# Output projection in plain fp32, and another warm-up of small matmuls, in a fused cross-attention and expert kernel

## Chip, cores and metric

One Trainium2 chip, one of its cores. The time is that of one execution on the device in microseconds; the kernel before ran three times.

## The reference

32 batches, each a matrix of 128 channels by 1024 positions, all fp32. A block of windowed cross-attention is followed by a mixture of rank-64 experts.

```
def xattn(x, cond, Wq, bq, Wk, bk, Wv, bv, Wo, bo):     # x: LayerNorm(x), cond: ctx
    q, k, v = Wq @ x + bq, Wk @ cond + bk, Wv @ cond + bv
    # 8 heads of 16 channels; position t sees the 16 keys from t-8 to t+7
    dots = einsum('bhdt,bhdtw->bhtw', qh, k_win) * hd ** -0.5
    out = einsum('bhtw,bhdtw->bhdt', softmax(dots), v_win)
    return Wo @ out + bo
x = x + xattn(layernorm(x), ctx, ...)
y = layernorm(x)
w = top-2 gate weights of softmax(y @ gate_w.T)          # 8 experts
x = x + sum over e of w[e] * (y @ A[e].T @ B[e].T)
```

## The kernel before

Every batch goes through one pipeline of five engines, each with its program written out by hand in the order of its instructions; semaphores join them. A step (`step(later, ahead, cur, prev, old)`) works on five batches at once: `later` is loaded and normalised, `ahead` gets its q and k projections and its first chunk of scores, `cur` its v projection, scores and softmax, `prev` its attention output and output projection `project_o`, and `old` the experts. `head` brings batches b0 to b3 to that point; then a step follows for each batch, the last ones with fewer batches. TensorE's program is unrolled in full (`loops=0`); the other engines loop over two steps.

Large products are made of float32r operands. A value is split in a high part, rounded to float32r (ScalarE, `*_hi`), and the rest (GpSimd or VectorE, `*_lo`), and `one_pass` multiplies high by high, high by low and low by high. `project_pass` does so for a 128x128 weight in `w_split` and half of 1024 columns, so a projection (`project_q`, `project_k`, `project_v`, `project_o`) is six float32r matmuls of 128x512 into `bank_c`. `down` (16 products, 128x264 or 128x256) and `up` (8 products, 128x512) are the experts' two matrices. The rest is plain fp32: a chunk of scores is 64 matmuls of 32x32, a chunk of weighted values 18 of 64x96 or less, and there are 12 transposes a batch. A plain fp32 statement other than a transpose stands in the profile as two matmuls and two weight loads: the 64 of a chunk of scores are x128, the 28 of the warm-up x56.

The order on TensorE in a step: v of `cur` (which waits for `x1_done`, the residual of `old`), weighted chunk 2 of `prev`, the first transposes, scores chunk 1, q of `ahead`, half of `down(0, ·)`, weighted chunk 3 of `prev`, the other half, scores chunk 2, half of `down(1, ·)`, weighted chunk 0 of `cur`, the other half, k of `ahead`, scores chunk 3, the second transposes, `project_o(prev)`, weighted chunk 1, half of `up`, scores chunk 0 of `ahead`, the other half of `up`. Each chunk opens with its waits (`open_scores`, `open_weighted`).

The attention output `attn` is written in four chunks, by ScalarE for even heads (`even_heads`) and by VectorE, which adds the odd ones (`join_heads`, `attn_done`). `attention_hi` (ScalarE, L676) and `attention_lo` (GpSimd, L1114) split it into `attn_split` for `project_o`. `even_heads(b, 0)` waits for `attn_lo` of the batch before, since it overwrites `attn`. VectorE's `residual` (L954) adds `project_o`'s result to x and `second_norm` follows it. At the end of the head, VectorE's order is `join_heads(b1, 0)`, `first_norm(b3)`, `residual(b0)`, `second_norm(b0)`, `scores_shift(b2, 0)`.

`warm_up(28)` runs 28 fp32 matmuls of 128x128 on a zeroed buffer before the data is there. SyncE issues the loads in a fixed order: x and ctx of b0, the constants, the weights in nine pieces (piece 0 holds Wq, Wk, Wv and Wo in 128x512), then `load_x(b1)`, which waits for `normal_lo(b0)` (L1120), and so on; in a step `place_v` (v_diag), `load_resid`, `load_x`, `load_ctx`, `store`.

Of the kernel before, what the change touches and what calls it, by code (L numbers as in the profile page):

```python
# [29 lines left out]
F32 = mybir.dt.float32  # L30
# [6 lines left out]
P = 128  # L37
# [7 lines left out]
KT = 32  # L45
# [53 lines left out]
def build(nc, x, ctx, wqkvo, biases, down_w, up_w, ident_in, mask_in, consts_in, out):  # L99
    with ExitStack() as stack:  # L100
        def sb(name, shape, dt=F32):
            return stack.enter_context(nc.sbuf_tensor(name, shape, dt))
# [4 lines left out]
        def sem(name):  # L107
            return stack.enter_context(nc.semaphore(name))
# [23 lines left out]
        attn = sb("attn", [P, T])  # L132
        attn_split = sb("attn_split", [P, 2, T], F32R)
        mid_split = sb("mid_split", [P, 2, T], F32R)
# [23 lines left out]


        small_in, consts_in_sbuf = sem("small_in"), sem("consts_in_sbuf")  # L160
        weights_in = [sem(f"weights_in{n}") for n in range(9)]
# [17 lines left out]
        exp_done, xt_hi = sem("exp_done"), sem("xt_hi")  # L179
        mask_set, ctx_hi, attn_hi = sem("mask_set"), sem("ctx_hi"), sem("attn_hi")  # L180
        xn_done, xn2_done = sem("xn_done"), sem("xn2_done")
# [7 lines left out]
        result_done, xt_lo = sem("result_done"), sem("xt_lo")  # L189
        attn_lo, rstd1, xn_lo = sem("attn_lo"), sem("rstd1"), sem("xn_lo")  # L190
        prob_done, rstd2, ctx_lo = sem("prob_done"), sem("rstd2"), sem("ctx_lo")
# [17 lines left out]
        def first(b):  # L209

            return isinstance(b.j, int) and b.j + b.c == 0
# [34 lines left out]
        def _(sp):  # L246
# [47 lines left out]
            def head(b0, b1, b2, b3):  # L294
# [7 lines left out]
                sp.dma_start(ident[:], ident_in).then_inc(small_in, 16)  # L302
                sp.dma_start(mask[:], mask_in).then_inc(small_in, 16)
                load_piece(2)
                load_piece(3)
# [34 lines left out]
        def _(pe):  # L340
# [126 lines left out]
            def project_o(b, free):  # L467

                pe.wait_ge(attn_hi, b.count(1, 1))
                pe.wait_ge(attn_lo, b.count(1, 1))  # L470
                pe.wait_ge(*free)
                for n in range(6):
                    last = project_pass(n, bank_c, 3, attn_split)
                    if n % 3 == 2:
                        last.then_inc(o_done, 1)

            def warm_up(matmuls):

                pe.wait_ge(prob_zero, 1)
                for n in range(matmuls):  # L480
                    nc.tensor.matmul(bank_c[:, 0:P], prob[:, 0:P], prob[:, 0:P], start=True, stop=True)

            def head(b0, b1, b2, b3):

                warm_up(28)
                first_masks()
# [40 lines left out]
            def step(later, ahead, cur, prev, old):  # L527
# [19 lines left out]
                if ahead:  # L547
                    project_q(ahead, (v_out, cur.count(1, 1)))
                pe.wait_ge(xt_lo, old.count(2, 1))
                if old.c == 0:  # L550
# [3 lines left out]
                if prev and cur:  # L554
                    open_weighted(prev, 3)
                    weighted_chunk(prev, 3)
                pe.wait_ge(xt_lo, old.count(2, 2))
                for f in range(4, FK):
# [20 lines left out]
                if cur:  # L579
                    project_o(prev, (k_out, ahead.count(1, 1)) if ahead else (v_out, cur.count(1, 1)))  # L580
                    open_weighted(cur, 1)
                    weighted_chunk(cur, 1)
                pe.wait_ge(ht_lo, old.count(1, 1))
                for e in range(EK):
                    up(0, e)
                if ahead:
                    pe.wait_ge(mask_set, ahead.count(CHUNKS, -1))
                    scores_chunk(ahead, 0)
# [7 lines left out]
        def _(act):  # L596
# [14 lines left out]
            def even_heads(b, m):  # L611

                act.wait_ge(pv_done, b.count(CHUNKS, m + 1))
                if m == 0 and b.c >= 1:
                    act.wait_ge(attn_lo, b.count(1, 0))
                src = bank_b[2 + m % 2][:].rearrange("p (n h i) -> p n h i", h=2, i=QT)
# [49 lines left out]
            def context_hi(b):  # L666

                act.wait_ge(ctx_in[b.parity], b.turn(1))
                nc.scalar.activation(ctx_split[:, 0, :], ctx_of(b), ACT.Copy).then_inc(ctx_hi, 1)  # L669

            def attention_hi(prev):

                act.wait_ge(attn_done, prev.count(CHUNKS, CHUNKS))
                if prev.c >= 1:
                    act.wait_ge(o_done, prev.count(2, 0))
                nc.scalar.activation(attn_split[:, 0, :], attn[:], ACT.Copy).then_inc(attn_hi, 1)  # L676

# [25 lines left out]
            def head(b0, b1, b2, b3):  # L703
# [41 lines left out]
                write_mask(b1, 2)  # L745
                attention_hi(b0)
                exponentials(b1, 3)
# [5 lines left out]
            def step(later, ahead, cur, prev, old):  # L753
# [19 lines left out]
                if prev:  # L773
                    even_heads(prev, 3)
                    attention_hi(prev)
                if cur:
# [293 lines left out]
        def _(pool):  # L1070
# [39 lines left out]

            def attention_lo(prev):

                pool.wait_ge(attn_hi, prev.count(1, 1))
                nc.gpsimd.tensor_tensor(attn_split[:, 1, :], attn[:], attn_split[:, 0, :].bitcast(F32),  # L1114
                                        ALU.subtract).then_inc(attn_lo, 1)

            def normal_lo(later):
# [5 lines left out]
            def head(b0, b1, b2, b3):  # L1123
# [22 lines left out]
                context_lo(b2)  # L1146
                attention_lo(b0)
                split_lo(7)
# [5 lines left out]
            def step(later, ahead, cur, prev, old):  # L1154
# [5 lines left out]
                if ahead:  # L1160
                    context_lo(ahead)
                if prev:
                    attention_lo(prev)
                if cur:
# [58 lines left out]
```

## Time and profile before

| | us |
|---|---|
| median of 3 runs | 1057.43 (1052.64 to 1060.89) |
| the profiled execution | 1057.9 |
| its span, first to last instruction | 1056.1 |
| TensorE matmul busy | 1011.5 (96%) |
| TensorE weight load busy | 869.8 (82%) |
| VectorE busy | 872.8 (83%) |
| ScalarE busy | 582.5 (55%) |
| GpSimd busy | 432.5 (41%) |

The mean granted clock of TensorE is 0.987 of full speed. A matmul's end is modelled and matmuls overlap in the pipeline, so the distance between two starts says more than the length of one. Idle time is shown in square brackets before an instruction, with what ended it; "issue" means that no wait is visible.

### The profile page before, as it was taken

How to read it: one execution, taken by the hardware profiler on the slowest of the kernel's cores; microseconds unless marked ns; L12 is line 12 of the kernel's file. 1: busy time of each engine (PE TensorE's matmuls, PEld its weight loads, DVE VectorE, ACT ScalarE, POOL GpSimd, SP SyncE). 2: the span in 40 equal slices, each digit the busy share in tenths (PEclk: the TensorE clock that was granted, in tenths of full speed). 3: DMA queues.
4: the chain of work that ended last, by engine and by line, in shares of the span. 5: the costliest groups of instructions: out<-in, count | busy, mean ns of one | idle time of the engine just before them, and what ended most of it. 6: DMA issues, size and time to landing. Idle time of an engine off the chain costs nothing.

```text
span 1056.1 us, 54652 instructions
## 1 busy us (share of the span) xinstructions
PE 1011.5 (96%) x24508; PEld 869.8 (82%) x24508; DVE 872.8 (83%) x1889; ACT 582.5 (55%) x812; POOL 432.5 (41%) x373
## 2 busy tenths in 40 slices
PE   6879999999999999999999999999999999999987
PEld 5768888888888888888888888888888888888866
DVE  3778888888888888888889888889888888888852
ACT  6666555556555556555555555556555555654420
POOL 7773434434434434343434343444343443443210
PEclk9899999999999999999999999999999999999998
DMA  7232333322333322223332223332233332222210
GB/s 271 78 80 86 83 84 103 103 66 81 82 83 103 103 81 71 76 84 103 103 85 71 84 83 91 103 103 58 87 84 83 103 103 73 76 81 64 64 41 40
DMA packets 157721, 92.47 MB, mean 88 GB/s; under 512 B 139728, under 2 KB 139856, under 8 KB 157520
## 3 DMA queue, kind: packets, MB, share of 16 engines
q1 hardware_dynamic: 157520, 89.25, 28.9%
q8 instruction: 192, 3.15, 1.2%
q14 instruction: 9, 0.07, 0.0%
HBM read 55.16 MB, written 16.78 MB: 68 GB/s over the span
## 4 chain that ended last, share of the span: by engine, by line
PE 87%; issue 5%; DVE 5%; ACT 2%; DMA 1%; POOL 1%; DVEq 0%; SPq 0%
PE bank_a L351 35%; PE bank_b L401 18%; PE bank_c L351 16%; PE bank_b L380 13%; PE bank_a L410 5%; DVE stats L815 1%; DMA raw<-x 1%; DMA prob_t<-ctx 0%; DVE h_sb L875 0%; DVE row_max L886 0%; DVE row_sum L900 0%; DVE pick L861 0%; DVE resid_pair L954 0%; POOL x_split L1120 0%; ACT x_split L688 0%
## 5 line engine op out<-in xcount | busy, mean ns | idle before, releaser
L401 PEld LDWEIGHTS bank_b<-prob_t,v_diag 64*64 64x64 f32 x4608 | 192.0, 134 | 50.3 <-issue 41.9
L401 PE MATMUL bank_b<-prob_t,v_diag 64*64 64x96 f32 (+2 forms) x4608 | 211.4, 239 | 12.6 <-issue 12.2
L351 PE MATMUL bank_a<-down_split,mid_split 128*128 128x264 f32 (+1 forms) x1536 | 213.7, 289 | 1.5 <-DVE mid_split L934 1.4
L351 PEld LDWEIGHTS bank_a<-down_split,mid_split 128*128 128x128 f32 x1536 | 193.4, 188 | 8.6 <-DVE mid_split L934 2.3
L1091 POOL TENSOR_TENSOR prob<-prob,row_inv 128x512 f32<-128x512 f32 x128 | 134.2, 1049 | 159.0 <-DVE row_inv L904 157.2
L351 PE MATMUL bank_a<-up_split,ht_split 128*128 128x512 f32 x768 | 196.6, 407 | 2.8 <-DVE ht_split L941 2.8
L380 PEld LDWEIGHTS bank_b<-k_sb,q_diag 32*32 32x32 f32 x16384 | 155.0, 105 | 43.9 <-issue 36.7
L380 PE MATMUL bank_b<-k_sb,q_diag 32*32 32x32 f32 x16384 | 170.6, 195 | 10.7 <-issue 6.7
L351 PEld LDWEIGHTS bank_a<-up_split,ht_split 128*128 128x128 f32 x768 | 142.8, 192 | 33.7 <-DVE ht_split L941 3.3
L1114 POOL TENSOR_TENSOR attn_split<-attn,attn_split 128x1024 fp32r<-128x1024 f32 x32 | 76.1, 2378 | 145.6 <-ACT attn_split L676 145.6
L913 DVE STREAM_TRANSPOSE prob_t<-prob 128x768 f32<-128x768 f32 x128 | 122.9, 961 | 0.9 <-POOL prob L1091 0.9
L624 ACT ACTIVATE prob<-prob 128x512 f32<-128x512 f32 x128 | 80.2, 627 | 67.0 <-DVE prob L892 67.0
L1120 POOL TENSOR_TENSOR x_split<-raw,x_split 128x1024 fp32r<-128x1024 f32 x32 | 76.9, 2404 | 96.5 <-ACT raw L688 96.5
L618 ACT ACTIVATE attn<-bank_b,consts 128x256 f32<-128x256 f32 x128 | 59.5, 465 | 90.1 <-PE bank_b L401 90.1
L886 DVE TENSOR_REDUCE row_max<-bank_b 128x16 f32<-128x512 f32 x128 | 86.7, 677 | 19.9 <-PE bank_b L380 19.5
L351 PE MATMUL bank_c<-ctx_split,w_split 128*128 128x512 f32 x372 | 98.6, 401 | 4.3 <-POOL ctx_split L1097 4.3
L1097 POOL TENSOR_TENSOR ctx_split<-raw,ctx_split 128x1024 fp32r<-128x1024 f32 x30 | 72.0, 2398 | 58.5 <-ACT ctx_split L669 58.5
L892 DVE TENSOR_TENSOR prob<-bank_b,row_max 128x512 f32<-128x512 f32 x128 | 88.5, 691 | 4.4
L900 DVE TENSOR_REDUCE row_sum<-prob 128x16 f32<-128x512 f32 x128 | 85.3, 666 | 2.1 <-ACT prob L624 1.9
L1105 POOL TENSOR_TENSOR rstd<-var_eps,consts 128x1 f32<-128x1 f32 x64 | 35.2, 550 | 124.9 <-DVE var_eps L824 124.9
L834 DVE SCALAR_TENSOR_TENSOR attn<-bank_b,consts,attn 128x256 f32<-128x256 f32 x128 | 58.3, 457 | 32.4 <-ACT attn L618 32.4
L351 PEld LDWEIGHTS bank_c<-ctx_split,w_split 128*128 128x128 f32 x372 | 68.8, 191 | 17.8 <-issue 4.3
(79 smaller groups left out, 1316.2 us busy)
## 6 DMA issues: line engine op xcount, KB each, us to landing
v_diag<-v_t SPq DMA_DIRECT2D x128, 132.0 KB, 3.3
raw<-x SPq DMA_DIRECT2D x32, 512.0 KB, 4.5
resid_pair<-x SPq DMA_DIRECT2D x32, 512.0 KB, 4.0
out<-resid_pair SPq DMA_DIRECT2D x32, 512.0 KB, 4.3
raw<-ctx SPq DMA_DIRECT2D x30, 512.0 KB, 3.3
stage<-down_w SPq DMA_DIRECT2D x2, 528.0 KB, 10.6
q_diag<-up_w SPq DMA_DIRECT2D x2, 512.0 KB, 5.7
prob_t<-up_w SPq DMA_DIRECT2D x2, 512.0 KB, 7.2
```

The source lines that it names most:

```text
L351: return nc.tensor.matmul(dst, st[:, s, st_cols], mv[:, m, mv_cols], start=start and n == 0, stop=stop and n == 2)
L380: last = nc.tensor.matmul(bank_b[m % 2][rows, t * KT:(t + 1) * KT], q_diag[rows, cur.parity, n, :], keys[rows, n * QT:n * QT + KT], start= ...
L401: last = nc.tensor.matmul(bank_b[2 + m % 2][rows, lo * PW:hi * PW], value_blocks(b)[rows, n, :], prob_t[rows, at:at + (hi - lo) * KT], sta ...
L624: nc.scalar.activation(weights_of(m), weights_of(m), ACT.Exp).then_inc(exp_done, 1)
L886: nc.vector.tensor_reduce(row_max[:, cols], scores, AX_X, ALU.max).then_inc(max_done, 1)
L892: nc.vector.tensor_tensor(weights_of(m), scores, row_max[:, cols].unsqueeze(2).broadcast_to([P, CT, KT]), ALU.subtract).then_inc(shifted, 1)
L900: nc.vector.tensor_reduce(row_sum[:, cols], weights_of(m), AX_X, ALU.add).then_inc(sum_done, 1)
L913: nc.vector.transpose(prob_t[:, m * PC:(m + 1) * PC], prob[:, m % 2 * PC:(m % 2 + 1) * PC]).then_inc(prob_t_done, 1)
L1091: nc.gpsimd.tensor_tensor(weights_of(m), weights_of(m), row_inv[:, cols].unsqueeze(2).broadcast_to([P, CT, KT]), ALU.mult).then_inc(prob_d ...
L1097: nc.gpsimd.tensor_tensor(ctx_split[:, 1, :], ctx_of(b), ctx_split[:, 0, :].bitcast(F32), ALU.subtract).then_inc(ctx_lo, 1)
L1114: nc.gpsimd.tensor_tensor(attn_split[:, 1, :], attn[:], attn_split[:, 0, :].bitcast(F32), ALU.subtract).then_inc(attn_lo, 1)
L1120: nc.gpsimd.tensor_tensor(x_split[:, 1, :], raw[:], x_split[:, 0, :].bitcast(F32), ALU.subtract).then_inc(xn_lo, 1)
```

## The change

The output projection takes `attn` and a plain copy `wo` of Wo as fp32 operands: two statements of 128x512, one for each half, instead of six float32r ones. `attn_split`, `attention_hi` and `attention_lo` are gone, and with them their passes on ScalarE and GpSimd. `wo` is loaded by a DMA of its own (128 rows of 512 bytes), issued after the mask and before piece 2. `project_o` waits for `attn_done`; `even_heads(b, 0)` waits for `o_done` of the batch before where it waited for `attn_lo`. The warm-up is 60 matmuls of 32 columns by 32 instead of 28 of 128 by 128. Four places on TensorE wait for more semaphores than before: both halves of `down(0, ·)` for `xt_hi` beside `xt_lo`, `up` for `ht_hi` beside `ht_lo`, and scores chunk 0 of `ahead` through `open_scores` for `k_out` and `q_out` beside `mask_set`.

```diff
+        wo = sb("wo", [P, P])
-        attn_split = sb("attn_split", [P, 2, T], F32R)
...
                 sp.dma_start(mask[:], mask_in).then_inc(small_in, 16)
+                sp.dma_start(wo[:], wqkvo[:, 3 * P:4 * P]).then_inc(wo_in, 16)
                 load_piece(2)
...
             def project_o(b, free):
-                pe.wait_ge(attn_hi, b.count(1, 1))
-                pe.wait_ge(attn_lo, b.count(1, 1))
+                pe.wait_ge(attn_done, b.count(CHUNKS, CHUNKS))
+                if first(b):
+                    pe.wait_ge(wo_in, 16)
                 pe.wait_ge(*free)
-                for n in range(6):
-                    last = project_pass(n, bank_c, 3, attn_split)
-                    if n % 3 == 2:
-                        last.then_inc(o_done, 1)
+                for n in range(2):
+                    half = slice(n * HALF, (n + 1) * HALF)
+                    nc.tensor.matmul(bank_c[:, half], wo[:], attn[:, half],
+                                     start=True, stop=True).then_inc(o_done, 1)
...
-                    nc.tensor.matmul(bank_c[:, 0:P], prob[:, 0:P], prob[:, 0:P], start=True, stop=True)
+                    nc.tensor.matmul(bank_c[0:KT, 0:KT], prob[:, 0:KT], prob[:, 0:KT], start=True, stop=True)
...
-                warm_up(28)
+                warm_up(60)
...
+                pe.wait_ge(xt_hi, old.count(2, 1))
                 pe.wait_ge(xt_lo, old.count(2, 1))
...
+                pe.wait_ge(xt_hi, old.count(2, 2))
                 pe.wait_ge(xt_lo, old.count(2, 2))
...
+                pe.wait_ge(ht_hi, old.count(1, 1))
                 pe.wait_ge(ht_lo, old.count(1, 1))
...
-                    pe.wait_ge(mask_set, ahead.count(CHUNKS, -1))
+                    open_scores(ahead, 0)
                     scores_chunk(ahead, 0)
...
                 if m == 0 and b.c >= 1:
-                    act.wait_ge(attn_lo, b.count(1, 0))
+                    act.wait_ge(o_done, b.count(2, 0))
```

The definitions and calls of `attention_hi` (ScalarE) and `attention_lo` (GpSimd) are removed in the head and in the step.

## Rows read from the trace of the kernel before

**Rows 1.** The summary: its span, queues, and the chain by engine.

```profile
span 1056.1 us, 54652 instructions
...
q8 instruction: 192, 3.15, 1.2%
...
PE 87%; issue 5%; DVE 5%; ACT 2%; DMA 1%; POOL 1%; DVEq 0%; SPq 0%
```

**Rows 2.** Windows: PE, PEld, DVE, ACT, POOL busy (count), clock, DMA share, GB/s.

```profile
480.00:580.00 100.00, 97.72 (x2469) 84.39 (x2469) 86.13 (x184) 57.28 (x80) 40.45 (x35) 1.00 0.31 89
```

**Rows 3.** All waits of TensorE from 80 to 1000 us.

```profile
PE bank_b L401 <- issue: 10.5, 19, 1.2
PE bank_b L380 <- issue: 2.4, 5, 0.8
PE bank_a L410 <- DVE h_sb L875: 1.0, 4, 0.3
```

**Rows 4.** Instructions in order of time, TensorE, one step: start us, us.

```profile
550.50 1.57 PE L401 MATMUL bank_b<-prob_t,v_diag 64*64 64x64 f32 x36
552.00 1.74 PE L351 MATMUL bank_a<-down_split,mid_split 128*128 128x264 f32 x12
553.67 1.29 PE L380 MATMUL bank_b<-k_sb,q_diag 32*32 32x32 f32 x128
...
556.49 0.66 PE L401 MATMUL bank_b<-prob_t,v_diag 64*64 64x64 f32 x10
557.69 1.23 PE L401 MATMUL bank_b<-prob_t,v_diag 64*64 64x96 f32 x26 [0.54 <-issue]
...
561.88 1.28 PE L380 MATMUL bank_b<-k_sb,q_diag 32*32 32x32 f32 x128
...
563.51 1.64 PE L351 MATMUL bank_c<-attn_split,w_split 128*128 128x512 f32 x6
565.08 1.58 PE L401 MATMUL bank_b<-prob_t,v_diag 64*64 64x64 f32 x36
566.58 3.02 PE L351 MATMUL bank_a<-up_split,ht_split 128*128 128x512 f32 x12
569.53 1.29 PE L380 MATMUL bank_b<-k_sb,q_diag 32*32 32x32 f32 x128
```

**Rows 5.** The same at the start: the masks' weight loads.

```profile
11.32 0.30 PEld L346 LDWEIGHTS bank_b<-mask,ident 128*128 128x128 f32 x2
...
11.86 0.19 PEld L346 LDWEIGHTS bank_b<-mask,ident 128*128 128x128 f32 x1 [0.24 <-issue]
...
12.29 0.19 PEld L346 LDWEIGHTS bank_b<-mask,ident 128*128 128x128 f32 x1 [0.24 <-issue]
```

**Rows 6.** The chain that ended last: start us, us, what.

```profile
12.30 8.28 DMA raw<-x
...
63.59 0.48 ACT attn L618
```

**Rows 7.** DMA issues of SyncE in the step of rows 4.

```profile
551.07 0.43 SPq L286 DMA_DIRECT2D resid_pair<-x  x1
551.83 0.34 SPq L270 DMA_DIRECT2D raw<-x  x1
```

**Rows 8.** Groups of instructions by line: count, busy us, mean ns, idle before.

```profile
L1114 POOL TENSOR_TENSOR attn_split<-attn,attn_split 128x1024 fp32r<-128x1024 f32 x32 | 76.1, 2378 | 145.6 <-ACT attn_split L676 145.6
...
L848 DVE CAST top_atf<-top_at 128x2 f32<-128x2 uint32 x32 | 67.8, 2120 | 1.1
```

**Rows 9.** Instructions in order of time, the tail.

```profile
1017.39 1.61 PE L351 MATMUL bank_c<-attn_split,w_split 128*128 128x512 f32 x6 [1.56 <-issue]
1018.43 1.41 DVE L954 SCALAR_TENSOR_TENSOR resid_pair<-bank_c,bias,resid_pair 128x512 f32<-128x512 f32 x2 [1.12 <-PE bank_c L351]
```

**Rows 10.** The same, TensorE, the last stretch of the head.

```profile
64.69 1.64 PE L351 MATMUL bank_c<-attn_split,w_split 128*128 128x512 f32 x6
...
67.76 1.65 PE L351 MATMUL bank_c<-ctx_split,w_split 128*128 128x512 f32 x6
```

More of the change, by code:

```diff
@@ L157, in build @@
         bank_c = psum("bank_c", T)
+        wo_in = sem("wo_in")
         small_in, consts_in_sbuf = sem("small_in"), sem("consts_in_sbuf")
@@ L179, in build @@
         exp_done, xt_hi = sem("exp_done"), sem("xt_hi")
-        mask_set, ctx_hi, attn_hi = sem("mask_set"), sem("ctx_hi"), sem("attn_hi")
+        mask_set, ctx_hi = sem("mask_set"), sem("ctx_hi")
         xn_done, xn2_done = sem("xn_done"), sem("xn2_done")
@@ L189, in build @@
         result_done, xt_lo = sem("result_done"), sem("xt_lo")
-        attn_lo, rstd1, xn_lo = sem("attn_lo"), sem("rstd1"), sem("xn_lo")
+        rstd1, xn_lo = sem("rstd1"), sem("xn_lo")
         prob_done, rstd2, ctx_lo = sem("prob_done"), sem("rstd2"), sem("ctx_lo")
@@ L669, in context_hi @@
                 nc.scalar.activation(ctx_split[:, 0, :], ctx_of(b), ACT.Copy).then_inc(ctx_hi, 1)
[L671 to L676, printed above, removed]
             def gap_exponential(old):
@@ L745, in head @@
                 write_mask(b1, 2)
-                attention_hi(b0)
                 exponentials(b1, 3)
@@ L774, in step @@
                     even_heads(prev, 3)
-                    attention_hi(prev)
                 if cur:
@@ L1109, in rows_norm @@
                                         rstd[:, which:which + 1], ALU.mult).then_inc(ready[1], 1)
[L1111 to L1115, printed above, removed]
             def normal_lo(later):
@@ L1146, in head @@
                 context_lo(b2)
-                attention_lo(b0)
                 split_lo(7)
@@ L1161, in step @@
                     context_lo(ahead)
-                if prev:
-                    attention_lo(prev)
                 if cur:
```

## Prediction

> **What bounds the kernel now.** I read the summary first. The chain that ended last is 87% TensorE, 5% "issue" and 5% VectorE, in a span of 1056.1 us [rows 1]. Then a window of the middle: in 100 us TensorE is busy 97.72 us at full granted clock, VectorE 86.13, ScalarE 57.28, GpSimd 40.45 [rows 2]. So between about 80 and 1000 us only two things move the end: what TensorE does, and the little time in which it does nothing. Third, the waits of that stretch: TensorE waited for another engine for 1.0 us in all, but 10.5 + 2.4 us for "issue", in 24 places [rows 3]. "Issue" is time in which no wait is visible. Fourth, one step in order of time: each group of matmuls follows the last without a gap, except that the 36 of `weighted_chunk(cur, 0)` break after the 10th [rows 4]. Ten of them take 10/36 of the 1.50 us that the whole group takes elsewhere (551.99 − 550.50), 0.42 us, and the eleventh starts 1.20 us after the first, so 0.78 us is lost where the view, whose matmul ends overlap, counts 0.54. With these 0.24 us more for each, the 24 gaps of [rows 3] are 12.9 + 24 × 0.24 = 18.7 us. A gap under 0.24 us isn't listed at all; I add 1.6 us for some ten steps that have one. That is 20.3 us, or 0.70 us in each of 29 steps.
>
> **What the gap is.** 192 instruction packets bring 3.15 MB [rows 1]: 16.4 KB each. TensorE has 24,508 matmuls and as many weight loads, 49,016 / 192 = 255 for a packet. So a packet is a block of 256 instructions of 64 bytes. From the code one step has 764 matmul records (24 for the four projections, 12 transposes, 48 down, 24 up, 512 scores, 144 weighted), hence 1,528 instructions; one more wherever a matmul waits for more than one semaphore (eight places: four `open_weighted`, q, k, o and the first transposes) makes 1,536 = 6 blocks exactly. That is why the gap stands behind the same 10th matmul in step after step. Going back 256 instructions from it (20 of the weighted chunk, 24 of `down`, 212 of scores) the block before began 44 instructions into scores chunk 2, at 553.67 + 0.21 = 553.88. The scores run at 256 instructions in 1.22 us, so this block is used up by 556.91, in 3.0 us, and the next is there at 557.69, 3.8 us after this one was entered. In this reading the next block is asked for on entry and takes 3 to 4.2 us (the upper end is the longest gap, 1.2 us, on 3.0). The other short block of a step ends in scores chunk 1 and has a few of the gaps, 2.4 us in all [rows 3].
>
> The Trainium skill ("Runtime: NRT & Kernel Launch", section "Instruction fetch mechanics") says that the sequencer fetches 16 KiB blocks of 256 instructions while it executes the current one, and that the cost is mostly hidden. By that rule, the trace agrees on the block and disagrees on the cost. The Trainium skill also gives TensorE room for 2,048 instructions, eight blocks, in the same section; with those filled ahead no gap would depend on one short block, which is the ground of a rival below.
>
> **The change, part by part.**
>
> 1. *`project_o` in plain fp32*: two statements, each two matmul records. The only fp32 matmuls of 128x512 are the two masks at the start: their weight loads stand at 11.86 and 12.29, so 0.43 us for each record at full clock [rows 5], 4 × 0.43 = 1.72 us. The six float32r passes are 0.23 us apart (`up`: twelve from 566.58 to 569.53, 2.95 us, with 0.1 to 0.2 of start-up), 1.38 us, and their group takes 1.57 us to the start of the next, 563.51 to 565.08 [rows 4]. The 0.19 us of start and end stay. So +0.34 us a batch, × 32 = +10.9 us. Bounds: +0.15 (1.72 against the whole 1.57) to +0.5 (if fp32 passes are slowed as float32r ones are, from 512 columns at 2.4 GHz, 0.213, to 0.23).
> The Trainium skill ("FP8 and Floating Point Precision", "TensorE Precision Notes") counts true fp32 as four passes. Eight passes at the measured 0.23 us would be 1.84 us, and the sum 3.8 us higher; the masks' rows speak for 1.72.
>
> 2. *Warm-up*: 60 statements are 120 records and 240 instructions, where 28 were 112. The sum of part 3 hangs on these +128. The 28 end at about 11.3 us, where the masks' loads begin [rows 5]; the small ones, at 0.04 to 0.06 us each by the scores (1.22 us for 128 in four row groups; half as fast at half the clock, at most), end some 2 to 4 us sooner. Then masks and first projections start up to 2 us earlier if the clock is up, or run at half speed. Both are covered: VectorE sits in `first_norm(b1)` for a load that is issued at 12.30 and takes 8.28 us [rows 6], and that load waits for `x_split`, which the warm-up doesn't touch. Without that cover a cold start could cost 1.3 us; I take 0, bounds −1 to +1.5.
>
> 3. *Instruction positions.* The step: `project_o` −4 instructions; the added second semaphores before both `down(0, ·)` halves, before `up` and before `scores_chunk(ahead, 0)` +4; `project_o` keeps one. It stays at 1,536, so block ends stay locked, but all move 123 to 125 instructions earlier (+128 warm-up, −4 in the first `project_o`). Back from the present gap by 124 is 79 instructions before the end of scores chunk 2: 554.5. The block before then begins 17 instructions into `weighted_chunk(prev, 3)`, 550.85 [rows 4]. The short blocks become 3.65 us (550.85 to 554.5) and 3.7 us (from 43 into scores chunk 3 to 24 into `weighted_chunk(cur, 1)`), instead of 3.0 and about as much; others are over 4.3. Against 3 to 4.2 us this leaves 0 to 0.55. But the first of them is asked for among the transfers of v_diag, resid and x (the last two issued at 551.07 and 551.83) [rows 7], where the long ones are likelier. I take 0.20 us a step for the gaps that stay, so −0.50 × 29 = −14.5 us. Bounds: none left (−20.3), as many as now (0). In the head the gaps move too; by the same count two go and one becomes two, so I take 0, ±2. The four added waits are for events long past, behind 1.5 us or more of queued matmuls: 0.
>
> 4. *`attention_hi` and `attention_lo` go*, a pass of ScalarE and one of 2.38 us on GpSimd a batch [rows 8]. In the steady stretch TensorE doesn't wait for them: 0. One by-effect: the 2-element cast L848 takes 2.12 us on average [rows 8], in which the GpSimd pass runs beside it; shortened, it takes away the waits for h_sb [rows 3], −1.0 us. In the tail TensorE stands 1.56 us for `attn_lo`, and `residual` starts at 1018.43 [rows 9]. Now `project_o` starts at 1015.8, its first half is out 0.09 + 0.43 + 0.6 later, at about 17.0, and VectorE, free of the long cast by then, starts 1.4 us earlier, but the second half comes 0.86 us after the first instead of 0.69: −1.2 us. What is late next is the chain of `residual`, `second_norm` and the gate on VectorE, unchanged.
>
> 5. *A new wait, `even_heads(b1, 0)` on `project_o(b0)`.* `attn` is now the operand itself, so ScalarE may overwrite it only after `project_o` of the batch before. In the steps that is long done. In the head it is not: TensorE's order is `weighted_chunk(b1, 0)`, `scores_chunk(b2, 0)`, `project_o(b0)`, and ScalarE's `even_heads(b1, 0)` runs at 63.59, before `project_o(b0)` begins at 64.69 [rows 6, 10]. The fourth record would start at 64.69 + 0.09 + 1.29 = 66.07 and end 0.6 later, so ScalarE goes at 66.75, 3.16 us later. Behind it on VectorE are queued `join_heads(b1, 0)`, `first_norm(b3)`, `residual(b0)`, `second_norm(b0)`, and TensorE's `project_v(b2)`, at 67.76, waits for `residual(b0)`. `even_heads(b1, 0)` is on the chain that ended last [rows 6]: +3.2 us, in full. Upper bound +5, if the clock falls in the 3 us that TensorE then stands.
>
> 6. *The load of `wo`*: 64 KB ahead of the weights; the load of x that ends the head comes behind it: the 512 KB of x take 8.28 us there [rows 6], an eighth of it would be 1.0; most of that is the queue ahead, so +0.3 us, bounds 0 to 1.
>
> Sum: the profiled execution took 1057.9 us, 1.8 more than its span and 0.5 over the median of three. 1057.9 + 10.9 − 14.5 − 1.0 − 1.2 + 3.2 + 0.3 = 1055.6; less 0.5, 1055.
>
> **The rivals.** *Slower: the gaps only move.* If the latency where the new short block is asked for is 4.3 us or more, 0.65 us remain of 0.70, and all gain is gone: 1055.1 + 13 = 1068, with fp32 at its upper bound 1073. For it: a gap of 1.2 us on 3.0 shows 4.2 us, and the loads stand just there. Against: in the step shown it took 3.8 [rows 4]. It decides from 4.3 us of latency on. The same time follows if the loading of instructions isn't the cause, and the gap belongs to `weighted_chunk(cur, 0)` itself. Beside this stands the skill's sentence on TensorE's eight buffered blocks; by it no gain from positions is to be had, and the time is this rival's. Together 0.2.
> *Faster: the gaps go, and the head doesn't pay.* −20.3 instead of −14.5, and fp32 at +0.25 a batch: 1055.1 − 5.8 − 2.9 = 1046. For it: 3.65 us is above most latencies seen. 0.15.
> *The small matmuls don't do a warm-up's work.* The clock is down for the first projections, and the cover of part 2 is short: 1057. Inside the forecast.
>
> **How the numbers follow.** 0.65 for the forecast, whose own range (gap left 0.05 to 0.45 us, fp32 ±0.1, head ±2) is 1048 to 1065. The unknown costs reach to both rivals, so the range is 1046 to 1069. One per cent, 10.6 us, is about what a measurement of this kernel tells from no change; faster than 1046.8 are most of the second rival and an edge of the forecast, 0.17; slower than 1068.0 some of the first, 0.18; between 0.65.
>
> **What would show it.** Right: `project_o` takes about 1.9 us to the next group in every step; breaks in groups of scores, none at the 10th matmul of `weighted_chunk(cur, 0)`; the waits for "issue" between 80 and 1000 under 6 us; the cast far below 2 us; `even_heads(b1, 0)` behind `project_o(b0)` and `project_v(b2)` near 71 us. The prediction is wrong if gaps stay above 0.5 us a step, if there are none, or if fp32 records stand more or less than 0.43 us apart.

## The result and the profile after

| | before | after |
|---|---|---|
| median | 1059.3 (1052.44 to 1062.8, 20 runs) | 1051.0 (1043.85 to 1053.75, 20 runs) |
| ratio of the two | | 0.9917 [0.9901, 0.9932] |
| profiled execution | 1057.9 | 1052.81 |
| its span | 1056.1 | 1050.9 |

Times are in microseconds; the ratio has its 95% interval in square brackets. The change makes the kernel 8.3 us or 0.8% faster. The forecast was 2.4 us or 0.2%. The profiled executions differ by less than the medians, 5.1 us: that of before lies 1.4 us under its median and that of after 1.8 us over its own. The summary of after, with its count of instruction packets and the chain by engine, against [rows 1]: "issue" has gone from 5% of the chain to 1%, VectorE from 5% to 2%.

```profile
span 1050.9 us, 54669 instructions
...
q8 instruction: 193, 3.16, 1.3%
...
PE 93%; ACT 2%; DVE 2%; DMA 1%; issue 1%; POOL 1%; SPq 0%; ACTq 0%
```

All waits of TensorE from 80 to 1000 us in after (total, times, longest). Against [rows 3], the 10.5 us in the weighted chunk are gone, and the waits for h_sb too; two long gaps in scores chunk 2 are new, 1.6 us at 337.36 and 2.0 us at 987.67.

```profile
PE bank_b L382 <- issue: 3.7, 2, 2.0
PE bank_a L353 <- issue: 0.6, 1, 0.6
PE bank_a L353 <- DVE mid_split L931: 0.2, 1, 0.2
```

TensorE in order of time in one step of after, to be laid beside [rows 4]. The weighted chunk at 555.62 is one group of 36 and no longer 10 and 26. `project_o` (L477) takes 563.64 − 561.83 = 1.81 us to the next group where six float32r passes took 1.57, and the transposes ahead of it 0.49 to the next start.

```profile
552.80 1.29 PE L382 MATMUL bank_b<-k_sb,q_diag 32*32 32x32 f32 x128
554.02 1.68 PE L353 MATMUL bank_a<-down_split,mid_split 128*128 128x256 f32 x12
555.62 1.58 PE L403 MATMUL bank_b<-prob_t,v_diag 64*64 64x64 f32 x36
...
561.34 0.66 PE L412 MATMUL bank_a<-ident,h_sb 128*128 128x128 f32 x4
561.83 1.88 PE L477 MATMUL bank_c<-attn,wo 128*128 128x512 f32 x4
563.64 1.58 PE L403 MATMUL bank_b<-prob_t,v_diag 64*64 64x64 f32 x36
```

The end of the head in after, TensorE and then ScalarE, against [rows 10] and the last of [rows 6]. `project_o` begins at 67.22 (before 64.69), `even_heads(b1, 0)` stands 4.71 us for its result, and `project_v(b2)` begins at 73.35 (before 67.76), 5.6 us later.

```profile
67.22 1.98 PE L477 MATMUL bank_c<-attn,wo 128*128 128x512 f32 x4
...
73.35 1.91 PE L353 MATMUL bank_c<-ctx_split,w_split 128*128 128x512 f32 x5 [2.64 <-DVE resid_pair L951]
...
69.30 0.47 ACT L624 ACTIVATE attn<-bank_b,consts 128x256 f32<-128x256 f32 x1 [4.71 <-PE bank_c L477]
```

The last full step and the tail in after, TensorE. Behind the gap at 987.67 12 matmuls take 2.24 us to the next group instead of 1.62 at 992.73, and the weighted chunk 2.42 instead of 1.51. `project_o` at 1012.11 has no wait ahead of it, against 1.56 in [rows 9].

```profile
984.66 1.00 PE L382 MATMUL bank_b<-k_sb,q_diag 32*32 32x32 f32 x95
987.67 0.47 PE L382 MATMUL bank_b<-k_sb,q_diag 32*32 32x32 f32 x33 [2.01 <-issue]
988.07 2.32 PE L353 MATMUL bank_a<-down_split,mid_split 128*128 128x256 f32 x12
990.31 2.49 PE L403 MATMUL bank_b<-prob_t,v_diag 64*64 64x64 f32 x36
992.73 1.69 PE L353 MATMUL bank_a<-down_split,mid_split 128*128 128x256 f32 x12
...
1012.11 1.88 PE L477 MATMUL bank_c<-attn,wo 128*128 128x512 f32 x4
```

Windows of after there (busy time of each engine and count, granted clock, DMA share, GB/s): the clock was 1.00 before the gap, and 0.66 in the five microseconds behind it.

```profile
980.00:988.00 8.00, 5.99 (x188) 5.49 (x187) 4.75 (x15) 1.89 (x4) 1.05 (x1) 1.00 0.53 125
988.00:993.00 5.00, 5.00 (x67) 4.69 (x53) 3.70 (x11) 0.63 (x1) 1.05 (x1) 0.66 0.02 3
```

When the starts of the two traces are laid side by side, after is 5.7 us late at 84 us of before, 8.0 us ahead at 970, 3.6 ahead once the step with the gap at 987.67 is over, and 5.2 ahead at the end. The middle gives it all.

### The profile page after: what moved, and what is told of

The parts are those of the page before. It is cut to its first block, busy times and chain, and to the rows that moved or that the text cites. A ratio compares the mean times of both kernels' runs of the same rounds, so it can differ in the third digit from the quotient of the medians.

```text
span 1050.9 us, 54669 instructions
## 1 busy us (share of the span) xinstructions
PE 1012.9 (96%) x24508; PEld 853.5 (81%) x24508; DVE 816.0 (78%) x1889; ACT 548.9 (52%) x780; POOL 357.6 (34%) x341
## 4 chain that ended last, share of the span: by engine, by line
PE 93%; ACT 2%; DVE 2%; DMA 1%; issue 1%; POOL 1%; SPq 0%; ACTq 0%
PE bank_a L353 37%; PE bank_b L403 18%; PE bank_b L382 15%; PE bank_c L353 13%; PE bank_c L477 5%; PE bank_a L412 5%; DMA raw<-x 1%; DMA prob_t<-ctx 0%; DVE stats L812 0%; POOL x_split L1111 0%; ACT x_split L687 0%; POOL ctx_split L1094 0%; ACT raw L687 0%; ACT q_diag L645 0%; ACT v_sb L662 0%
## 5 line engine op out<-in xcount | busy, mean ns | idle before, releaser
L403 PE MATMUL bank_b<-prob_t,v_diag 64*64 64x96 f32 (+2 forms) x4608 | 205.1, 241 | 0.0
L653 ACT ACTIVATE k_sb<-bank_c,bias 128x1024 f32<-128x1024 f32 x31 | 34.5, 1113 | 104.3 <-PE bank_c L353 104.2
```

Of the source, the lines that this page charges most:

```text
L403: last = nc.tensor.matmul(bank_b[2 + m % 2][rows, lo * PW:hi * PW], value_blocks(b)[rows, n, :], prob_t[rows, at:at + (hi - lo) * KT], sta ...
```

## The experiments

Thirteen runs of twelve kernels. Ratios are to the kernel before on the same chip. "Step" is the mean distance between the same instruction of neighbouring steps.

| run | what it is | median | ratio |
|---|---|---|---|
| a1_warm_only | before, 60 small matmuls | 1048.5 | 0.9912 [0.9889, 0.9935] |
| a3_filler | before, 28 large and 32 tiny | 1048.0 | 0.9922 [0.9895, 0.9948] |
| a2_fp32_old_warm | after, 28 large matmuls | 1058.83 | 1.0021 [1.0, 1.0043] |
| a4_drift | after, without its four added waits | 1077.63 | 1.0195 [1.0168, 1.0223] |
| b4_after_with_passes | after, split passes kept | 1059.0 | 1.0035 [1.0011, 1.0059] |
| b1_late_split | a1, split passes issued later | 1037.32 | 0.9814 [0.9789, 0.984] |
| b2_late_split_old_warm | before, split passes later | 1058.11 | 1.0003 [0.9977, 1.003] |
| b3_two_attn | after, two attn buffers | 1049.07 | 0.9929 [0.9905, 0.9953] |
| c3_b1_again | b1 once more | 1039.43 | 0.9815 [0.9777, 0.9852] |
| c1_tail | b1, old order in the tail | 1037.96 | 0.9803 [0.9768, 0.9838] |
| c2_68 | b1, 68 small matmuls | 1033.85 | 0.9775 [0.9733, 0.9818] |
| d1_80 | b1, 80 small matmuls | 1059.52 | 1.0012 [0.9987, 1.0036] |
| d2_tail_68 | c1 and c2 together | 1031.06 | 0.9744 [0.9715, 0.9773] |

**The warm-up alone, and instructions that only take up room (a1_warm_only, a3_filler).**

```diff
 # a1, on before
-nc.tensor.matmul(bank_c[:, 0:P], prob[:, 0:P], prob[:, 0:P], start=True, stop=True)
+nc.tensor.matmul(bank_c[0:KT, 0:KT], prob[:, 0:KT], prob[:, 0:KT], start=True, stop=True)
...
-warm_up(28)
+warm_up(60)
 # a3, on before: warm_up(28) stays large, and behind it
+for n in range(32):
+    nc.tensor.matmul(bank_c[0:KT, 0:KT], prob[:, 0:KT], prob[:, 0:KT], start=True, stop=True)
```

> The kernel before, with only the warm-up changed (60 small matmuls, 128 instructions more). Theory (gaps come from the loading of instruction blocks, and the warm-up only moves the block ends): the gaps behind the 10th matmul of weighted chunk 0 are gone, 'issue' waits of TensorE from 80 to 1000 us under 4 us where they were 12.9, and no fp32 or head cost is paid: 0.980 to 0.985 of before, about 1040. Rival (fp32 operands or the dropped passes made the gaps go): same as before, within 0.3%.

> The kernel before, with its 28 large warm-up matmuls and 32 tiny ones behind them: the same 128 instructions more as 60 small ones, with a longer warm-up. Theory of positions: gaps gone as in a1_warm_only, 0.980 to 0.987 of before. Rival (what helps is a shorter warm-up): same as before or slower by 1 to 2 us.

Both give the same time, 0.8 to 0.9% less, so it is the 128 added instructions and not the size of the matmuls. That is as much as the whole change gives (0.9917), and less than I expected of either (0.980 to 0.987). The gaps of a1 in the weighted chunk are gone, but a new wait has come. The waits of TensorE from 80 to 1000 us in a1_warm_only:

```profile
PE bank_a L410 <- DVE h_sb L875: 8.5, 21, 0.4
PE bank_b L380 <- issue: 2.7, 7, 0.8
```

Its instructions in order of time show where that comes from. GpSimd's `attention_lo` starts at 517.78, VectorE's cast of two elements 0.19 us later, and the cast lasts 2.23 us, to the end of the pass. Everything behind it on VectorE is late, h_sb (L875, the experts' hidden values times the gate's `pick`) included, and the transposes stand for it.

```profile
517.78 2.39 POOL L1114 TENSOR_TENSOR attn_split<-attn,attn_split 128x1024 fp32r<-128x1024 f32 x1 [4.49 <-ACT attn_split L676]
517.97 2.23 DVE L848 CAST top_atf<-top_at 128x2 f32<-128x2 uint32 x1
...
525.45 0.69 DVE L875 TENSOR_TENSOR h_sb<-bank_a,pick 128x256 f32<-128x256 f32 x2
...
526.19 0.66 PE L410 MATMUL bank_a<-ident,h_sb 128*128 128x128 f32 x4 [0.39 <-DVE h_sb L875]
```

**The projection alone (a2_fp32_old_warm).** On after: `warm_up(28)` with 128x128 matmuls, as before.

> The kernel after, with the 28 large matmuls back as warm-up. Theory: block ends stand again within a few instructions of where they were, the gaps come back (12 to 20 us), and the costs of the fp32 projection (10.6) and of the wait in the head (3) stay: 1.008 to 1.013 of before. Rival (the gain is from the dropped passes and the shorter cast): 0.992, as after.

With the old count the gaps are back at the weighted chunk. The waits from 80 to 1000 us:

```profile
PE bank_b L403 <- issue: 8.5, 22, 0.7
PE bank_a L353 <- issue: 1.1, 1, 1.1
PE bank_a L353 <- DVE mid_split L931: 0.2, 1, 0.2
```

The ratio is below what I expected. By groups, over the 28 steps between 84 and 970 us of before, `project_o` and the transposes ahead of it cost 9.2 us more, as priced; but the weighted chunks give back 4.3, scores chunk 1 gives back 4.1, and the waits for h_sb 1.8. The positions had moved by a few instructions (the gap stands behind the 12th matmul and not the 10th), and the cast is short. It is not a pure price of the projection.

**Positions that drift (a4_drift).** Without the four added waits a step has 1,532 instructions, and the block ends lie four instructions later from step to step.

```diff
 # on after
-pe.wait_ge(xt_hi, old.count(2, 1))
...
-pe.wait_ge(xt_hi, old.count(2, 2))
...
-pe.wait_ge(ht_hi, old.count(1, 1))
...
-                    open_scores(ahead, 0)
+                    pe.wait_ge(mask_set, ahead.count(CHUNKS, -1))
```

> The kernel after without its four added semaphore waits on TensorE (all are implied by others), so that a step has 1532 instructions and block ends move 4 instructions from step to step. Theory: no gap in the first ten steps, growing ones up to 2 to 3 us around the 20th step where one block holds nothing but scores, in all 20 to 35 us: 1.01 to 1.025 of before, slower than after though work was taken away. Rival (the waits cost their 51 ns each, positions don't matter): 0.985 to 0.992.

It held. Early steps have hardly a gap, and from about the tenth on one grows to 2 us and wanders from the scores into `down` and the weighted chunk. The waits from 80 to 1000 us, and below them, in order of time, one gap, three matmuls before the end of a chunk of scores:

```profile
PE bank_b L382 <- issue: 9.8, 9, 1.9
PE bank_a L353 <- issue: 6.3, 6, 1.6
PE bank_b L403 <- issue: 1.9, 2, 1.0
```

```profile
655.52 0.32 PE L382 MATMUL bank_b<-k_sb,q_diag 32*32 32x32 f32 x3 [1.91 <-issue]
```

So the four waits, which do nothing for the data, are worth 29 us (1.0195 − 0.9917 of 1057) to the change. They keep the step at 1,536 instructions. In every trace with such gaps, their places counted in TensorE's instructions (a matmul and its weight load are two, and each extra wait is one more) are 193 modulo 256.

**What the split passes cost (b4_after_with_passes, b1_late_split, b2_late_split_old_warm).** b4 is after with `attention_hi` and `attention_lo` in their old places, their results unused. b1 is a1 with the passes a little later; b2 is the same move on before.

```diff
 # b1, on a1 (b2, on before): ScalarE
                     even_heads(prev, 3)
-                    attention_hi(prev)
                 if cur:
                     write_mask(cur, 1)
                 if old:
                     gap_exponential(old)
+                if prev:
+                    attention_hi(prev)
...
 # GpSimd
-                if prev:
-                    attention_lo(prev)
                 if cur:
                     weights_norm(cur, 1)
+                if prev:
+                    attention_lo(prev)
```

> The kernel after with the two split passes of attn still done, their result unused. Theory: the cast is long again and TensorE waits for h_sb, but the fp32 projection has itself taken 0.33 us of the 0.34 us by which VectorE's step is longer, so only 2 to 6 us are lost against after: 0.994 to 0.998 of before, h_sb waits of 1 to 6 us. Rival (dropping the passes gives as much as a1_warm_only lost to h_sb, 8 to 10 us, whatever the projection takes): 1.000.

> The kernel before with 60 small warm-up matmuls (as a1_warm_only), and the split of attn moved behind the gate: ScalarE does attention_hi after gap_exponential, GpSimd attention_lo after weights_norm(cur, 1), so that the GpSimd pass no longer runs beside the cast L848. Theory (with the gaps gone, the steps of a1_warm_only wait for h_sb on VectorE, because the cast takes 2.1 us beside that pass): the cast falls under 1.2 us, the waits of TensorE for h_sb under 1 us where they were 8.5, steps of 30.7 us instead of 31.04, 0.979 to 0.985 of before, some 8 us faster than a1_warm_only. Rival (VectorE is bound by its own work, not by the cast): as a1_warm_only, 0.991.

> The same move of the split with the old warm-up. Theory: the gaps of 0.7 us a step cover VectorE's lateness, so the shorter cast is worth little here: 0.995 to 1.000 of before, h_sb waits (1.0 us) gone. Rival (the cast costs the same in both): 0.988 to 0.992.

In b4 my own theory fell and its rival held: the passes alone cost 12.5 us (1.0035 − 0.9917 of 1057), all of the change's gain. The groups (busy us, mean ns) and waits of b4_after_with_passes show the long cast and the wait for h_sb in 25 steps:

```profile
L857 DVE CAST top_atf<-top_at 128x2 f32<-128x2 uint32 x32 | 67.6, 2114 | 1.1
```

```profile
PE bank_a L414 <- DVE h_sb L884: 8.7, 25, 0.4
```

I had thought that the fp32 projection's longer step would absorb that wait. It doesn't. I put that down to h_sb's lateness counting from `down(0, ·)` of the same step, ahead of `project_o`; no run tests it.

b1 held: 20 us less than before, with float32r kept. `attention_lo` starts 2.2 us later in the step than in a1 (6.25 us ahead of the transposes of h_sb, and 8.41 there; medians). In b1_late_split the cast runs before ScalarE has freed `attention_lo`:

```profile
513.46 0.17 DVE L849 CAST top_atf<-top_at 128x2 f32<-128x2 uint32 x1
...
513.86 1.04 ACT L676 ACTIVATE attn_split<-attn 128x1024 fp32r<-128x1024 f32 x1
...
514.98 2.37 POOL L1115 TENSOR_TENSOR attn_split<-attn,attn_split 128x1024 fp32r<-128x1024 f32 x1 [3.53 <-ACT attn_split L676]
```

b2 held too: while the gaps are there the same move is worth nothing. The gap, 0.7 to 0.8 us a step in before, stands between `down(0, ·)` and h_sb's readers, and hides the cast. The two gains don't add; the second exists only once the first is taken. Step: before 31.40 us, b2 31.32, a1 31.04, b4 31.37, after 30.99, b1 30.63.

**The wait in the head (b3_two_attn).** After with two attn buffers by the parity of the batch, so that `even_heads(b1, 0)` has nothing to wait for.

```diff
 # on after; every reader and writer takes attn[b.parity]
-        attn = sb("attn", [P, T])
+        attn = [sb("attn0", [P, T]), sb("attn1", [P, T])]
...
-                if m == 0 and b.c >= 1:
-                    act.wait_ge(o_done, b.count(2, 0))
+                if m == 0 and b.c >= 2:
+                    act.wait_ge(o_done, b.count(2, -2))
```

> The kernel after with two attn buffers in turn, so that even_heads waits for the project_o of two batches before. Theory (the wait of even_heads(b1, 0) for project_o(b0) is 3 to 4 us of the head): project_v(b2) starts 3 to 4 us earlier than in after, at about 69.5 to 70.5, and the time is 0.987 to 0.990 of before, 2.5 to 4 us less than after. Rival (VectorE or the load of x holds the head anyway): as after, 0.992.

In its trace, TensorE and then ScalarE, `even_heads(b1, 0)` runs at 64.97 and `project_v(b2)` at 70.08, 3.3 us before after's 73.35:

```profile
66.66 1.99 PE L477 MATMUL bank_c<-attn,wo 128*128 128x512 f32 x4
...
70.08 1.66 PE L353 MATMUL bank_c<-ctx_split,w_split 128*128 128x512 f32 x6
...
64.97 0.47 ACT L624 ACTIVATE attn<-bank_b,consts 128x256 f32<-128x256 f32 x1 [0.77 <-PE bank_b L403]
```

The ratio missed the 0.987 to 0.990 that I expected, and the rival's "as after" fits it (0.9929 against 0.9917, intervals overlapping). Of the 3.3 us, 0.6 were there before `project_o` began (66.66 against 67.22), so the wait is worth 2.7. In the profiled pair b3 stays 2.3 us or more ahead of after from 84 to 970 us; that this reaches the median is not shown.

**What makes a gap (c2_68, d1_80).** b1 with 68 and with 80 small matmuls, and b1 again.

```diff
-                warm_up(60)
+                warm_up(68)    # c2_68
+                warm_up(80)    # d1_80
```

> b1_late_split with 68 small matmuls ahead of the first data instead of 60: 32 more instructions, no other edit. By the count of instructions every block end lies 32 instructions earlier in the step; with the starts of b1_late_split's trace the two shortest blocks of a step are then used up in 1.47 us and 2.9 to 3.0 us, where they take 3.30 and 3.72 us in b1_late_split. Theory (a block of 256 instructions is asked for when the one before is entered and takes some 3 to 4 us to be there): new gaps of 1.5 to 2.5 us behind the block of 1.47 us and of 0.1 to 1.0 us behind the other, in every step, 1.6 to 3.3 us a step, so 45 to 95 us more than c3_b1_again: 1082 to 1132 us, a ratio of 1.023 to 1.07. Rival (several blocks are fetched ahead, and only their mean rate counts; the gaps before had another cause that the count of 60 happens to avoid): no more than 5 us of difference to c3_b1_again, a ratio of 0.979 to 0.986.

> The same text as b1_late_split, to stand beside c1_tail and c2_68 on one chip: a ratio to the kernel before of 0.979 to 0.984 as in its first run.

Here the rule of my prediction fell. c2_68 has a block of 256 instructions that is used up in about 1.5 us in every step, and not one gap behind it; it is no slower than b1 on the same chip (1033.85 against 1039.43, intervals overlapping). Its whole list of waits from 80 to 1000 us is one line, and that is the tail's wait for `attention_lo`:

```profile
PE bank_c L351 <- issue: 4.7, 1, 4.7
```

The trace holds the packets of the instruction queue, 16,384 bytes each. From 418 to 428 us, in 40 slices, c2_68's DMA moved three of them (slices 2, 19 and 37: they start at 418.3, 422.6 and 427.1) and next to nothing else. Below it TensorE in the same stretch:

```profile
GB/s 49 82 0 0 0 0 0 0 0 0 0 0 0 0 0 0 0 0 66 0 0 0 0 0 0 0 0 0 0 0 0 0 0 0 0 0 66 0 0 0
...
q8 instruction: 3, 0.05, 2.0%
```

```profile
422.40 1.56 PE L351 MATMUL bank_c<-ctx_split,w_split 128*128 128x512 f32 x6
423.88 1.29 PE L380 MATMUL bank_b<-k_sb,q_diag 32*32 32x32 f32 x128
425.11 0.66 PE L410 MATMUL bank_a<-ident,h_sb 128*128 128x128 f32 x4
```

The short block runs from the first scores, 423.9, to 425.5. The block behind it came with the packet of 422.57, which starts 1.4 us before execution enters the short one. So it isn't execution that asks. Something ahead of it does; I take it for TensorE's sequencer, which would be ahead while slow float32r matmuls wait in line, and have no lead behind scores. That is inferred: no row shows where the sequencer stood. d1_80 was chosen to tell this from the view that short blocks don't matter at all.

> b1_late_split with 80 small matmuls ahead of the first data: block ends 80 instructions earlier than there, and 48 earlier than in c2_68, whose block of 1.47 us left no gap, so that the rule of the earlier runs (the next block is asked for when execution enters the one before) fell. Its trace shows that this block was asked for 2.3 us before execution entered the one ahead of it, while TensorE's sequencer stood 30 to 50 instructions ahead in slow float32r matmuls. Revised theory (asked for when the sequencer enters; that is early behind float32r matmuls and not early behind scores or transposes): here the two shortest blocks are 2.32 us, entered in the transposes behind weighted chunk 2 with at most 0.6 us of lead, and 3.79 us, entered inside a chunk of scores with none; against 3.3 to 4.0 us from asking to executing that leaves 0.4 to 1.2 us a step, 12 to 35 us in all: 1049 to 1074 us, a ratio of 0.992 to 1.013. Rival (several blocks are buffered and short ones are no cause of gaps at all): within 5 us of c3_b1_again, a ratio of 0.977 to 0.986.

It held. The waits of d1_80 from 80 to 1000 us, and one step of it: a break behind the 114th matmul of scores chunk 1, in 29 steps. By my recount the block before it is entered in the last matmuls of weighted chunk 2, at 513.8, just ahead of the transposes. The "2.3 us" for c2_68 in the text above is a guess at the moment of asking; the packet itself starts 1.4 us ahead.

```profile
PE bank_b L380 <- issue: 17.0, 29, 0.9
```

```profile
514.09 1.09 PE L410 MATMUL bank_a<-ident,xn 128*128 128x128 f32 x8
515.11 1.17 PE L380 MATMUL bank_b<-k_sb,q_diag 32*32 32x32 f32 x114
517.01 0.32 PE L380 MATMUL bank_b<-k_sb,q_diag 32*32 32x32 f32 x14 [0.72 <-issue]
```

Corrected as in the prediction (17.0 + 29 × 0.24) that is 24 us; the median is 20 to 22 us over b1's. In its trace the packets in front of these gaps start 0.5 to 1.1 us after the block before is entered, take 0.9 to 1.3 us, and the first instruction runs 1.2 to 1.6 us after they are in: 2.8 to 3.4 us from entering to entering. In before the same sum is 3.4 to 4.5 us, near the 3 to 4.2 that the prediction read off. What is new is that the packet can also start before the block is entered: by 0.9 to 1.8 us for the short block of c2_68, by up to 2.6 in a4_drift. Before's own trace had it too: behind the block that is entered in weighted chunk 2, just after the float32r matmuls of `project_v`, ten packets start up to 0.6 us ahead of that entry.

Long gaps also come in some executions and not in others. c3_b1_again is the text of b1, where no "issue" gap in the scores is over 0.5 us; its profiled execution took 1043.14 us against 1036.95, with a gap of 1.96 us at 332.42 and a granted clock of 0.66 from 333 to 338 us. The longest of its waits in the scores is the last number here (80 to 1000 us):

```profile
PE bank_b L380 <- issue: 3.3, 3, 2.0
```

**The tail, and all together (c1_tail, d2_tail_68).** b1 moved the passes in the last steps too, where the cast loses little beside them (it took 0.77 us at 1016.55 in before); there TensorE waited 4.68 us for `attention_lo`. c1 keeps the old order in steps without `cur`; d2 is c1 with 68.

```diff
 # c1, on b1: ScalarE; GpSimd's attention_lo likewise
                     even_heads(prev, 3)
+                    if not cur:
+                        attention_hi(prev)
...
-                if prev:
+                if cur and prev:
                     attention_hi(prev)
```

> b1_late_split, but in the steps that have no batch in place of cur (the tail) the two split passes stand in their old places, since nothing there runs beside VectorE's cast. In b1_late_split TensorE stood 4.68 us at 999.67 for attention_lo in the last step but one. Theory (that wait is on the chain that ends last, and after the old order's 1 to 2 us wait nothing else is late): 2 to 4 us less than c3_b1_again in the same call, a ratio to the kernel before of 0.977 to 0.980. Rival (the tail's end is set by VectorE's chain of residual, second_norm and gate, and the wait only moves): less than 1 us of difference to c3_b1_again.

> c1_tail with 68 small matmuls ahead of the first data, the two edits together that were each the fastest here. Theory (the tail's shorter wait for attention_lo is worth its 3 us and c2_68's positions cost nothing): 1029 to 1034 us, a ratio of 0.973 to 0.978. Rival (the tail's wait is off the chain that ends last or is given back to a lower clock there): 1034 to 1038 us, a ratio of 0.978 to 0.982.

The wait in the tail falls from 4.68 to 1.56 us. The medians say 1.5 us for it (c1 against c3, same chip), less than their spread: not settled. In c1 the transposes of h_sb then wait 1.90 us for VectorE, where c2_68's wait 0.52. And in c1's profiled execution the up products of the tail take 8.21 us, where c2_68's take 5.74, at a granted clock of 0.70 against 1.00 (windows of c1_tail, then c2_68), so some of the gain can be given back there. In d2_tail_68 they take 7.32 us.

```profile
1006.00:1015.00 9.00, 8.65 (x28) 6.71 (x28) 1.38 (x2) 0.67 (x2) 0.00 (x0) 0.70 0.00 0
```

```profile
1004.00:1010.00 6.00, 5.97 (x28) 4.93 (x28) 0.88 (x2) 0.38 (x1) 0.00 (x0) 1.00 0.00 0
```

d2_tail_68 has the lowest median of the study: 1031.06 us, 0.9744 [0.9715, 0.9773], 2.6% under before and 1.7% under after, with the projection in float32r.

## Why the prediction was right or wrong

The time, 1051.0, lies in the range and within the 1% for which 0.65 was given, but the gain is more than three times the forecast: 8.3 us and not 2.4. That the time is only 4 us off the 1055 is partly luck, since before's median over twenty runs is 1.9 us above that of three. By its steps, in the profiled pair:

- *Projection in fp32.* The records stand 0.43 us apart, as forecast. `project_o` costs 1.81 − 1.57 = 0.24 us more and not 0.34, since its group ends 0.1 us sooner than I added; the transposes ahead of it cost 0.08 more (0.49 against 0.41), which I didn't foresee. That the total, 0.33 a batch or 10.5 us, is so near 10.9 is luck in part.
- *Gaps.* The step that failed, as the prediction put it: "I take 0.20 us a step for the gaps that stay, so −0.50 × 29 = −14.5 us." The place of the gaps and the effect of +124 instructions were right. Between 84 and 970 us of before (28 steps) weighted chunk 0 took 19.3 us less and scores chunk 1 took 4.3 less: before had 23.6 us of gaps there, and not 20.3. Scores chunk 2, where the gap moved to, took 2.4 us more, 0.08 a step and not 0.20. So the term was −21.2 us, beyond its far bound of −20.3. Behind it is the rule that the next block is asked for on entry. The block that I feared, asked for among the loads of v_diag and x, is entered behind `down`, and its packet starts 0.54 us after entry in the median, where that of before's short block starts after 1.11. c2_68 shows that rule wrong. The corrected one foretold d1_80.
- *The split passes.* "In the steady stretch TensorE doesn't wait for them: 0", and −1.0 for the cast. The mechanism was named and its size was wrong. With the gaps in place it is worth nothing (b2); without them 12.5 us (b4). I took the waits for h_sb from a trace in which the gaps hid them. The forecast hardly suffered (−1.8 measured in scores chunk 3), as it never added these waits as what is late next; had the passes stayed, it would have been over 10 us too low. The change's gain needs both halves.
- *The head.* The new wait cost what was forecast: `project_v(b2)` lost 5.6 us, of which 2.5 were there before `project_o` began, so 3.1 against 3.2. b3 gives 2.7 of it back. The 2.5 are the term that was too small (+0.3 for the load and 0 ± 2 for the head's gaps): the load of x(b1) took 9.41 us instead of 8.28, and I put the rest down to gaps at other places. The load took 8.97 in a1, which has no load of `wo`, and 8.73 in b3, which has one, so `wo` isn't shown to be the cause.
- *Warm-up.* Right, 0 for its size: a3 with large and a1 with small matmuls agree.
- *Tail.* −1.2 forecast; −1.6 measured, with the projection's own +0.3 in it. Not foreseen was the last full step: of its 4.4 us, 3.7 are a gap of 2.0 us and the clock of 0.66 behind it, and 0.7 the projections of two steps. It is the block that I feared: the packet in front of the gap started 3.2 us after the block before was entered, at 985.24, when the loads had kept the DMA engines 94 to 97% busy from 982 to 985; it took 0.9 us, as most do. So what was late was the start of the packet. b3 has such a gap of 2.1 us in the same step.

In the profiled pair the sum is +5.7 in the head, −13.7 in the middle, +4.4 in the last full step, −1.6 in the tail: −5.2, as in the spans. The middle is −21.2 for the gaps, +9.2 for the projection (28 steps), −1.8 of waits for h_sb, and 0.1 for the rest. The forecast's sum for this pair was −2.3. The other 3 us of the medians' 8.3 are the places of the two profiled executions in their spreads, and no trace divides them.

The rival "the gaps only move" is out for this change, but d1_80 and a4_drift show that it is real at other counts. The rival "the gaps go and the head doesn't pay" was half right: nearly all gaps went, and the head paid in full. The Trainium skill ("Runtime: NRT & Kernel Launch", "Instruction fetch mechanics") gives TensorE room for 2,048 instructions, eight blocks. Filled ahead, they would leave no gap behind one short block; the 29 gaps of d1_80 speak against that. In our traces one packet is fetched for each block, and between 90 and 970 us it is in at most 6.0 us, and at least 1.1 us, before the block is entered.

Open stays what sets the sequencer's lead: I inferred it from the packets' starts and have no row of the sequencer itself. The account isn't complete either: a1's block entered 20 matmuls into a chunk of scores has the next packet start 0.55 us before entry (median), and before's block entered 25 matmuls into one (scores chunk 0) has it start 2.3 us after. Open is also whether the tail's and the head's 3 us reach the median.

## What to carry to other kernels

In an unrolled program the count of instructions before the steady loop, and the length of a step modulo 256, are parameters like any tile size: look for "issue" gaps at the same instruction in every step, and try a few counts of instructions that do nothing. When a gap or a wait goes, ask which wait it was hiding before you price the other halves of the change: here the slow cast was worth 0 or 10 to 12 us. And price an engine's small instructions by what runs beside them: moving a pass by 2 us gave 10 us (a1 to b1), near the 12.5 that removing it gave (b4 to after), and without the 10.5 us of fp32 that the removal cost.

## What the runs showed that I had not expected

- A cast of 128x2 elements on VectorE takes 0.17 us alone and mostly 2.2 us (up to 2.4) when GpSimd's 128x1024 subtraction starts just ahead of it; it ends with that pass. Where it runs ahead of the pass, as in b1, another small one takes its place: `pick` (L862, 128x8) takes 785 ns on average there and 302 in a1. Three small ones ahead of it there keep their 0.14 to 0.21 us. b1 has no wait of TensorE for h_sb from 80 to 1000 us.
- Twenty more matmuls on zeros, 80 instructions, turned b1's ratio of 0.9815 into 1.0012; eight more gave 0.9775, whose interval overlaps that of b1.
- After TensorE stood still for 2.0 us in after's last full step, the granted clock was 0.66 over the next 5 us, so 1.2 GHz for two thirds of them and 2.4 for the rest. The gaps of at most 0.9 us in d1_80 left it at 1.00 (480 to 580 us), and so did the gap of 1.6 us at 337.36 in after (337 to 342 us). Behind c3_b1_again's 1.96 us it was 0.66 again (333 to 338 us).
